# Chunk outputs of a Mamba-2 scan with tokens on the partitions, and the decays of its windows made beside the convolution

## What is computed

```python
z, xBC, dt = split(_rms(x, norm_w) @ in_proj_w)      # 512, 768, 8 channels
dt = softplus(dt + dt_bias)
xBC = silu(conv_b + sum(padded[:, k:k + L, :] * conv_w[:, k] for k in range(4)))
xh, Bm, Cm = split(xBC)                               # 8 heads x 64, 128, 128
def step(h, inp):                                     # over 512 tokens
    dec, u, bt, ct = inp                              # dec = exp(dt * A), u = dt * xh
    h = h * dec[:, :, None, None] + u[..., None] * bt[:, None, None, :]
    y = jnp.einsum('bhpn,bn->bhp', h, ct)
    return (h, y)
y = ys + D_skip * xh
out = x + _rms(y * silu(z), gnorm_w) @ out_proj_w
```

## Time and profile before

| | |
|---|---|
| time, median of 3 runs | 9226.33 us (9217.38 to 9246.14) |
| time of the profiled execution | 9249.62 us |
| its span | 9247.8 us |
| PE busy | 7938.6 us (86%) |
| PEld busy | 3524.7 us (38%) |
| DVE busy | 5014.7 us (54%) |
| ACT busy | 3326.8 us (36%) |
| POOL busy | 1960.8 us (21%) |
| mean granted clock of TensorE | 0.897 |

### The profile page before, as it was taken

How to read it: one execution, slowest core, us unless ns; L and a number is a source line. 1 busy time by engine, 2 the same in 40 slices (tenths; PEclk the granted TensorE clock), 3 DMA queues, 4 the chain that set the end, 5 groups by cost and what they waited for, 6 DMA issues and landing times.

```text
span 9247.8 us, 129067 instructions
## 1 busy us (share of the span) xinstructions
PE 7938.6 (86%) x37700; PEld 3524.7 (38%) x38020; DVE 5014.7 (54%) x12781; ACT 3326.8 (36%) x4038; POOL 1960.8 (21%) x1802
## 2 busy tenths in 40 slices
PE   3979799897998979889798897979989798897988
PEld 0343433434333343333434334343343433334343
DVE  3555364654645556454564656536465464555546
ACT  0424334242342424424243342433424234242442
POOL 3040130302203031130311304013030221303113
PEclk5989889898998989989799898989989899898998
DMA  3142231323313132041422303223131330313213
GB/s 73 20 74 35 41 60 20 65 33 48 53 19 70 28 57 51 12 75 23 69 39 26 71 17 69 35 43 57 20 69 30 50 58 12 70 28 64 45 19 72
DMA packets 216597, 421.47 MB, mean 46 GB/s; under 512 B 35542, under 2 KB 126584, under 8 KB 215812
## 3 DMA queue, kind: packets, MB, share of 16 engines
q1 hardware_dynamic: 213841, 412.14, 25.9%
q10 hardware_dynamic: 2048, 0.53, 0.0%
HBM read 190.14 MB, written 8.51 MB: 21 GB/s over the span
## 4 chain that ended last, share of the span: by engine, by line
PE 59%; issue 14%; DVE 13%; DMA 6%; POOL 4%; ACT 2%; SPq 2%; DVEq 0%; ACTq 0%; POOLq 0%
PE ps L1004 13%; PE ps L941 10%; PE ps L975 8%; PE ps L977 6%; PE ps L903 5%; DVE mx L1588 5%; PE ps L979 4%; PE ps L1009 4%; DMA stage<-in_mask 3%; PE ps L1124 2%; DMA qst<-q1hl 2%; PE ps L960 2%; PE ps L1040 2%; DVE xc L1716 1%; ACT PR L1362 1%
## 5 line engine op out<-in xcount | busy, mean ns | idle before, releaser
L1362 ACT ACTIVATE PR<-ps 128x1024 f32<-128x1024 f32 x2496 | 2504.0, 1025 | 2634.8 <-PE ps L977 1514.2
L1559 DVE CUSTOM_DVE_ANT_0 ps<-ps,maskq 128x402 f32<-128x402 f32 x4203 | 2408.3, 587 | 1567.1 <-PE ps L941 1375.8
L1004 PE MATMUL ps<-PR,vbuf 128*32 128x512 f32 x9984 | 1356.6, 616 | 5.2 <-ACT PR L1362 5.2
L977 PE MATMUL ps<-maskk,identb 128*128 128x512 bf16 x3008 | 1147.6, 382 | 0.0
L941 PE MATMUL ps<-kst,qst 96*128 96x402 bf16 (+1 forms) x3115 | 1026.0, 342 | 115.6 <-DVE mx L1559 89.9
L1588 DVE TENSOR_REDUCE mx<-ps 128x2 f32<-128x804 f32 x1024 | 933.3, 988 | 314.1 <-PE ps L960 312.7
L960 PE MATMUL ps<-kst,qst 100*128 100x402 f32 x2048 | 753.3, 495 | 360.8 <-DMA qst<-q1hl 254.4
L975 PE MATMUL ps<-qst,kst 99*128 99x512 bf16 x2496 | 956.7, 383 | 7.3
L979 PE MATMUL ps<-qst,kst 102*128 102x512 f32 x1664 | 768.0, 526 | 100.3 <-ACT PR L1362 71.0
L941 PEld LDWEIGHTS ps<-kst,qst 96*128 96x128 bf16 x3115 | 282.4, 97 | 1209.7 <-DVE mx L1559 819.4
L722 POOL MEMSET qst<- 3x2048 f32 (+1 forms) x34 | 47.5, 1398 | 3117.7 <-PE ps L1004 3071.1
(11 more groups left out here) (194 smaller groups left out, 8046.4 us busy)
## 6 DMA issues: line engine op xcount, KB each, us to landing
kst<-khl SPq DMA_DIRECT2D x96, 800.5 KB, 17.0
kst<-khl SPq DMA_DIRECT2D x300, 200.1 KB, 7.6
stage<-in_maskt SPq DMA_DIRECT2D x204, 256.0 KB
stage<-in_mask SPq DMA_DIRECT2D x204, 201.0 KB
ctxs<-in_ctxt SPq DMA_DIRECT2D x17, 1601.0 KB, 9.7
qst<-q1hl SPq DMA_DIRECT2D x96, 256.0 KB, 12.1
win_s<-in_w_in SPq DMA_DIRECT2D x16, 1288.0 KB, 5.9
KS<-khl SPq DMA_DIRECT2D x102, 200.1 KB
```

The lines of the kernel that those rows point to most:

```text
L977: mm = pe.matmul(o, identb[:, :], maskk[:, t, :], start=False, stop=True)
L1004: mm = pe.matmul(ps[32 * j:32 * j + 32, 6, :], l, PR[:, t % 2, j, :], start=(t == 0), stop=(t == KT - 1), tile_position=(0, 32 * j))
L1362: nc.scalar.activation(PR[:, t % 2, 2 * half:2 * half + 2, :], ps[:, 2 * half:2 * half + 2, :], ACT.Exp, scale=scale).then_inc(s_p, 1)
L1559: nc.vector.tensor_tensor_reduce(src, src, maskq[:, i, c0:c0 + w], 1.0, -3.0e38, ALU.add, ALU.max, mx[:, c, h * QT + i:h * QT + i + 1]).th ...
```

## The change

The chunk's output is now computed with tokens on the partitions. The 8 matmuls of a chunk have the window (128 x 128) as weights and 64 columns of `dx` to stream, and all write one bank. The state's part is one matmul (`s_zi`), scaled afterwards by a third column group of `dec`, so `Ce`, its exponential and its matmuls go. The skip term D x becomes four matmuls with a diagonal `dskd`. z is projected with tokens on the partitions as well. The gated output `ug` is squared by ACT with an accumulator, transposed by PE, copied by ACT and projected, block by block inside the chunk loop; the norm's one-column matmuls go.

All four `window_sums` and exponentials stand in the loop of the input projection; the windows lie in the space of `QS1`, and two DMAs (`rows_q1`) restore the constant rows there. Eight fills stand ahead of the transposes, one behind each j from 0 to 9 and three behind j = 10. The exponential of dt is ahead of the copies on ACT, and the convolution has three DVE instructions, as ACT makes the fourth tap. POOL makes the first four key parts after the RMS scale, and the rest between and behind the four `spread_a`. The LayerNorm has three DVE passes in place of four (with the square sum), and its RMS scale is made in two halves. The second LayerNorm, the transposes and q are split in three tiles and one. `spread` has four matmuls over all 128 rows, with no wait among them, and stands behind the first tile of `project_out`. On SP two mask pieces are loaded before x, and the other two after `stack_q1`.

```diff
+OUT_BANK = [5, 7, 6, 3]
+XT1_BANK = [2, 4]
+FILL0 = V_LN + 1
+FILL_AT = [1] * (NCH + XT) + [3]
+assert FILL0 + sum(FILL_AT) == KT + 2 * NC
...
+    def rows_q1(b):
+        sp.wait_ge(s_yp, LEAD + (b + 1) * QT)
+        alone(sp)
+        for g in range(G1):
+            sp.dma_start(f(QS1[g][KROWS1:MROW1 + 1, :, :]), qrows1.rearrange("r (h t) -> r h t", h=GH))\
+                .then_inc(s_qs1[g], 16)
...
-        sp.wait_ge(s_g, QT * (b + 1))
+        load_pieces(b, bn, 0, PIECE1, False)
+        sp.wait_ge(s_D, QT * (b + 1))
         alone(sp)
         load_xt(bn)
-        load_pieces(b, bn, 0, PIECE1, False)
         sp.wait_ge(s_vfree, (b + 1) * KT)
         alone(sp)
         load_ctx(bn)
+        rows_q1(b)
         for g in range(G1):
             stack_q1(b, g)
...
         def spread_a(c):
+            pool.wait_ge(s_a, b + 1)
             if c > 0:
                 pool.wait_ge(s_D, b * QT + c)
-                if c > 1:
-                    pool.wait_ge(s_cum, b * (QT - 1) + c - 1)
             nc.gpsimd.tensor_tensor(
                 aU[:, :, :], aa[:, c, :].unsqueeze(2).broadcast_to([P, HM, P]),
                 upto[:, :].unsqueeze(1).broadcast_to([P, HM, P]), ALU.mult).then_inc(s_au, 1)
         spread_a(0)
-        for c in range(QT):
+        spread_a(1)
+        spread_a(2)
+        parts(b, K1[NC])
+        spread_a(3)
+        for item in K1[NC + 1:]:
+            parts(b, item)
...
-        project_out(wo0_s, 0, G0 - 1, G0, G0 - 1)
-        fill(1)
+        project_out(wo0_s, 0, G0 - 1, G0, range(1))
+        spread(b, G0 - 1)
+        project_out(wo0_s, 0, G0 - 1, G0, range(1, QT))
         pe.wait_ge(s_norm, LEAD + b * NG + G0)
         project_out(wo0_s, G0 - 1, G0, G0)
-        fill(1)
-        fill(NC - 2 + V_LN)
+        fill(FILL0)
...
-            if j == NCH + 1:
+            if j == 4:
                 whole_decays(b)
-            elif j == NCH + 2:
-                window_sums(b, 0)
-            if j == 4:
                 pe.wait_ge(s_sp, b * SPN + 1)
...
             mm.then_inc(s_in, 1)
-        fill(V_IN)
+            fill(FILL_AT[j])
+            if NCH - 2 <= j < NCH + 2:
+                window_sums(b, j - NCH + 2)
+        assert not second
+        pe.wait_ge(s_xc, b * NCH + 2)
+        pe.wait_ge(s_vfree, (b + 1) * KT)
+        pe.wait_ge(s_rest, rests(b, K1[-1]) + 1)
+        for c in range(QT):
+            cs = slice(c * P, (c + 1) * P)
+            mm = pe.matmul(ps[:, 6, cs], xc[:, NCH - 2, cs], xc[:, NCH - 1, cs], start=True, stop=True)
+        mm.then_inc(s_G, 1)
+        for c in range(QT - 1):
+            cs = slice(c * P, (c + 1) * P)
+            mm = pe.transpose(ps[:, 7, cs], xc[:, NCH - 2, cs], ident[:, :])
+        mm.then_inc(s_bt, 1)
+        def x_tokens(c):
+            if c == 0:
+                pe.wait_ge(s_zs, b * XT + 1)
+                pe.wait_ge(s_xc, NCH * (b + 1))
+            else:
+                pe.wait_ge(s_dx, b * QT + c)
+            for i in range(XT):
+                mm = pe.transpose(ps[:, 1, i * P:(i + 1) * P], xc[:, i, c * P:(c + 1) * P], ident[:, :])
+            mm.then_inc(s_tok, 1)
+        def project_block(c):
+            pe.wait_ge(s_g, b * QT + c + 1)
+            if c == 0:
+                pe.wait_ge(s_zs, XT * (b + 1))
+            else:
+                pe.wait_ge(s_ut, b * QT + c)
+            for i in range(XT):
+                mm = pe.transpose(ps[:, 0, i * P:(i + 1) * P], ug[:, c % 2, i * P:(i + 1) * P], ident[:, :])
+            mm.then_inc(s_gt, 1)
+            pe.wait_ge(s_ut, b * QT + c + 1)
+            if c == 0:
+                pe.wait_ge(s_Ld, QT * (b + 1))
+            elif c == 1:
+                pe.wait_ge(s_btok, b + 1)
+            elif c == 2:
+                pe.wait_ge(s_GM, b + 1)
+            for k in range(XT):
+                mm = pe.matmul(ps[:, OUT_BANK[c], 0:D], yt[:, k, c * P:(c + 1) * P], wout_s[:, k, :],
+                               start=(k == 0), stop=(k == XT - 1))
+            mm.then_inc(s_op, 1)
+        x_tokens(0)
         for c in range(QT):
             cs = slice(c * P, (c + 1) * P)
             nb = b * QT + c
             if c > 0:
-                window_sums(b, c)
+                pe.wait_ge(s_h, LEAD + b * (QT - 1) + c)
+                if c == 1:
+                    pe.wait_ge(s_zs, b * XT + 3)
+                else:
+                    pe.wait_ge(s_ti, b * (QT - 1) + c - 1)
+                pe.matmul(ps[:, 3, :], xc[:, NCH - 1, cs], Hst[:, :], start=True, stop=True).then_inc(s_zi, 1)
...
+                pe.wait_ge(s_zs, b * XT + 2)
+                pe.wait_ge(s_dskd, b + 1)
+            elif c == 1:
+                pe.wait_ge(s_g, nb)
+            else:
+                pe.wait_ge(s_tj, b * (QT - 1) + c - 1)
             for i in range(XT):
...
-            fill(1)
+                pe.matmul(ps[:, 2, i * P:(i + 1) * P], xc[:, i, cs], dskd[:, i, :], start=(i == 0), stop=False)
             pe.wait_ge(s_M, nb + 1)
             pe.wait_ge(s_dx, nb + 1)
...
             for h in range(HM):
-                i, e = h // 2, h % 2
-                o = ps[64 * e:64 * e + 64, 2, i * P:(i + 1) * P]
-                mm = pe.matmul(o, dx[:, h * PD:(h + 1) * PD], Ld[:, h, :], start=True, stop=(c == 0),
-                               tile_position=(0, 64 * e))
-                if c > 0:
-                    mm = pe.matmul(o, Hst[:, h * PD:(h + 1) * PD], Ce[:, h, :], start=False, stop=True,
-                                   tile_position=(0, 64 * e))
+                mm = pe.matmul(ps[:, 2, h * PD:(h + 1) * PD], window(c)[:, h, :], dx[:, h * PD:(h + 1) * PD],
+                               start=False, stop=(h == HM - 1))
             mm.then_inc(s_yp, 1)
             if c < QT - 1:
+                x_tokens(c + 1)
...
+                pe.matmul(ps[:, 4, :], btok[:, c, :], dx2[:, :], start=True, stop=True).then_inc(s_hp, 1)
+            if c > 0:
+                project_block(c - 1)
+        pe.wait_ge(s_ti, (b + 1) * (QT - 1))
+        project_block(QT - 1)
...
+                mm = pe.transpose(ps[:, XT1_BANK[k], i * P:(i + 1) * P], xs1[:, i, k * P:(k + 1) * P], ident[:, :])
+            if i >= QT - 2:
+                mm.then_inc(s_xst1, 1)
+            if i == QT - 2:
+                pe.wait_ge(s_xn1, 2 * DT * b + DT)
+                for item in LASTQ:
+                    project_q1(item, 0, i * P + P)
+        pe.wait_ge(s_xn1, 2 * DT * (b + 1))
         for item in LASTQ:
-            project(b, item, pj_bank[item], None)
+            project_q1(item, (QT - 1) * P, T).then_inc(s_proj, 1)
...
     def window_decays(b, c):
-        nb = b * QT + c
-        act.wait_ge(s_D, nb + 1)
-        act.wait_ge(s_yp, LEAD + nb)
-        nc.scalar.activation(Ld[:, :, :].rearrange("p h t -> p (h t)"),
+        act.wait_ge(s_D, b * QT + c + 1)
+        nc.scalar.activation(window(c).rearrange("p h t -> p (h t)"),
                              ps[:, 4:6, :].rearrange("p a n -> p (a n)"), ACT.Exp).then_inc(s_Ld, 1)
...
+            nc.scalar.activation(xc[:, ch, :], ps[:, bank, :], ACT.Identity, bias=cb_c[:, ch:ch + 1],
+                                 scale=cw_c[:, ch * TAPS + TAPS - 1:(ch + 1) * TAPS])
             nc.scalar.activation(rawc[:, n % 2, TAPS - 1:TAPS - 1 + T], ps[:, bank, :], ACT.Copy)\
                 .then_inc(s_rawcp, 1)
...
+        act.wait_ge(s_sp, b * SPN + 2)
+        nc.scalar.activation(sp_t[:, 2, :], sp_t[:, 1, :], ACT.Exp).then_inc(s_spe, 1)
...
+        for n in range(NCH):
+            gate(n)
+            if n + 2 < NCH:
+                copy_raw(n + 2)
+            fill(FILL_AT[n + 3])
+            if n == 0:
+                act.wait_ge(s_dps, b + 1)
+                nc.scalar.activation(dec[:, :, :].rearrange("p a n -> p (a n)"),
+                                     ps[:, 4, 0:3 * QT * HM], ACT.Exp).then_inc(s_dec, 1)
+            elif n <= QT:
+                window_decays(b, n - 1)
...
+        for c in range(QT):
             act.wait_ge(s_g, b * QT + c + 1)
-            cs = slice(c * P, (c + 1) * P)
-            nc.scalar.activation(zs[:, :, cs], yt[:, :, cs], ACT.Square).then_inc(s_g2, 1)
...
+            nc.scalar.activation(th[:, c % 2, :], ug[:, c % 2, :], ACT.Square, accum_out=ssq[:, c:c + 1])\
+                .then_inc(s_g2, 1)
+            act.wait_ge(s_gt, b * QT + c + 1)
+            nc.scalar.activation(yt[:, :, c * P:(c + 1) * P], ps[:, 0, :].rearrange("p (a n) -> p a n", a=XT),
+                                 ACT.Copy).then_inc(s_ut, 1)
...
         for i in range(QT):
+            nc.vector.scalar_tensor_tensor(out=xres[:, i, :], in0=xres[:, i, :], scalar=moments[:, i, 0:1],
+                                           in1=lng_s[:, :], op0=ALU.subtract, op1=ALU.mult).then_inc(s_ln[0], 1)
+        dve.wait_ge(s_rstd, b + 1)
+        dve.wait_ge(s_ln[0], QT * (b + 1))
+        for i in range(QT):
```

## The result

The changed kernel takes 8695.89 us (median of 4 runs, 8694.80 to 8698.13) against 9225.26 us (4 runs of the kernel before; the 9226.33 of the table ahead is the median of three of them): a ratio of 0.942, 95% interval 0.941 to 0.944. The profiled execution spans 8693.3 us, so its 16 batches take 543.3 us each against 578.0 before, 34.7 less.

A forecast was written before the change was run, and what follows sets the result against it. The prediction took PE as the bound (59% of the chain) and counted its waits: 10.0 - 18.7 + 18.3 + 8.7 + 5.8 = 24.1 us a batch, 386 in 16, so 9226 - 386 = 8840 us, range 8640 to 9000.

The forecast's parts named there:

- Head: Layer 0's end to dt: covered reciprocal, shorter spread, LayerNorm by tiles; 10.0 us a batch gained, bounds 8 and 12.
- Projection and convolution: Layer 1's input projection: PE the bound, ACT's fifth key waits for the stack; 18.7 us a batch lost, bounds 3 and 25.
- Scan and tail: First scan matmul to q ready: chunks of 8.5 us for 11.4; 18.3 us a batch gained, bounds 10 and 24.
- the 3 us for a low clock: Scan and tail: allowance for a low clock in the tail and narrow matmuls in the chunks, raising 46.1 to 49.1 us.
- The fear that narrow matmuls bring the clock down: Rival: PE falls to 1.2 GHz from the scan to q, 34 us more a batch, 9384 us; chance 0.04.
- q: PE's wait for q's DMAs: context and two mask pieces leave their way; 8.7 us a batch gained, bounds 4 and 12.
- The rest: Batch's end and layer 0's groups: shorter spreads, covered reciprocal, clock; 5.8 us a batch gained, bounds 3 and 8.
- The stack lands in time: Rival beside the convolution: key stack there when ACT needs it, 11.0 us a batch given back, 8665 us; chance 0.15.
- The clock stays at 2.4 GHz: Rival: no low PE clock in the convolution, scan and tail, 9.9 us a batch given back, 8682 us; chance 0.15.
- Chunks stay a chain, or q waits for the context: Rival: chunks take 11.4 us, or the context delays q; 8.7 us a batch lost either way, 8980 us; chance 0.19.

The follow-up runs named there:

- key_less: Changed kernel with the last of the first key stack's three DMAs copying one head of four (a quarter of its bytes): 8601.0 us.
- k_last: Changed kernel with the second four key projections behind all values and POOL's fourth window-sum input ahead of their parts: 8555.4 us.
- win_half: Changed kernel with each of the scan's 64 window matmuls streaming 32 columns instead of 64: 8867.2 us.
- before_sp: Kernel before the change, with only SP's queue altered: context issued once the values are taken, two mask pieces instead of four ahead of q: 9156.5 us.
- narrow: Changed kernel with the spread of the reciprocals back to 32 rows, one row group after the other: 8922.6 us.
- no_cover: Changed kernel with all of `project_out` behind the spread again, in both layers: 8773.6 us.
- rms_once: Changed kernel with POOL's first half of the RMS norm waiting for the squares of all four tiles: 8779.0 us.
- ctx_late: Changed kernel with the context issued behind the constant rows, directly ahead of q's wait, some 25 us later: 8696.6 us.

## Why the prediction was right, and where it was not

*Head, 10.0 forecast, 12.8 measured.* The reciprocal, the spread and `project_out` were counted at 3.4. From the last group's sums to DVE's first addition the head took 13.6 us before and 7.2 after, so 6.4. The prediction left out the clock: it was 0.75 in this stretch before and is 1.00 after:

```profile
2689.70:2703.32 13.62, 12.28 (x47) 9.63 (x48) 1.64 (x2) 0.39 (x1) 0.58 (x2) 0.75 0.00 0
```

```profile
2542.36:2549.53 7.17, 7.17 (x43) 6.29 (x44) 1.64 (x2) 0.00 (x0) 0.00 (x0) 1.00 0.00 0
```

The LayerNorm by tiles was closer: from that addition to the transposes 17.6 us before and 10.5 after, 7.1 less where 5.6 was counted; from there to dt it grew by 0.7, where 1.0 less was counted.

*Projection and convolution, -18.7 forecast and measured.* The mechanism is right: PE is the bound, the fifth key waits for the stack, POOL's fourth input is queued behind it, PE's fourth window sum behind that, and this sum starts 43.0 us into the stretch, where 43.1 was counted. (The fourth key part's terms there, 9.8, 4.4 and 2, add up to 16.2 and not 16.4.) That the loss agrees to a tenth is luck. PE reaches the wait 2 us sooner, so the stall is 10.4 us for 8.5, and PE's work outside it takes 47.4 us where 49.8 was counted, 42.7 of instructions and 7 for the clock. `key_less` and `k_last` show that the stall is real and is worth 8.8 us a batch. The Trainium skill ("DMA: Bandwidth & Descriptors", section Bandwidth) has 341 GB/s for 1 MB from HBM to 128 partitions; by an estimate from this figure the stack would land in 7 us. The trace does not agree for this transfer, which goes from SBUF to 32 partitions: its last DMA landed 22.3 us after its issue, with 2.4 MB in all. The context is a transfer from HBM; it landed in 6.8 us when nothing ran beside it, 1601 KB or 241 GB/s.

*Scan and tail, 18.3 forecast, 23.1 measured.* A chunk takes 7.9 us where 8.5 was counted (its terms add up to 8.4), and the fourth block is projected 33.8 us into the stretch, not 35.4. From there to the end of q are 10.6 us, and 10.7 were counted before the 3 us for a low clock. So these 3 us are the larger mis-sized term: the clock is 1.00 in the scan and 0.96 over the whole stretch. The fear that narrow matmuls bring the clock down was not wrong but early, as `win_half` shows.

*q, 8.7 forecast, 6.8 measured.* The queue on SP is the cause (`before_sp`), and PE's wait for q's DMAs is 9.7 us and not 8.

*The rest, 5.8 forecast, 11.7 on the mean.* This is the term that was sized worst. It had 4.2 us for shorter spreads and a covered reciprocal and 1.6 for the clock. By the means of the batches the groups of layer 0 gained 5.8 us, the part of layer 1 behind its first scores 3.3, and the first scores themselves 2.6, where nothing was counted. In these three stretches together PE's time at half fell from 52 to 38 us a batch. That is worth at most half, 7 us, where 1.6 was counted, and 4.2 + 7 is close to the 11.7. Over the whole batch the time at half fell from 119 to 79 us; 5 of these 40 lie in the wait for q, where PE is idle and they cost nothing. `narrow`, `no_cover` and `rms_once` show the same thing backwards: a microsecond of wait or of narrow matmuls put back costs two to four. No run holds the clock and changes only the instructions, so the split between the two stays an estimate.

*The rivals.* "The stack lands in time" gave 8665, nearer to the measured time than the forecast's 8840, and it is wrong: ACT waits 11.3 us. "The clock stays at 2.4 GHz" (8682) is the nearer in kind, but only the 3.0 us that it had in the scan and tail came in part; beside the convolution the clock stayed low (0.85), and where it rose, in the head and in the rest, little or nothing was counted. "Chunks stay a chain, or q waits for the context" is excluded by the 7.9 us and by `ctx_late`. Whoever checks this forecast by its total alone would pick the wrong story: 8696 comes from a stall that exists and a clock gain that was not counted.

## What to carry to other kernels

Before a wait or a narrow form is priced by its own microseconds, look at PE's clock in the stretches behind it: here each microsecond of wait or of narrow matmuls put back cost two to four. When a move makes one engine wait in program order for a DMA, list what is queued behind it on that engine; taking the second four key projections behind the values, with no byte less, took a 10 us stall away. And judge a forecast by its stretches, not by its sum.

## What the runs showed of the hardware that was not expected

- Less streaming made PE slower: 32 instead of 64 columns in 64 matmuls with full weights left each at 0.117 us at full clock, and the clock fell from 1.00 to a mean of 0.80 in the scan shown (`win_half`).
- The context's DMA landed after 25.7 us when it was issued behind the second key stack, 7.3 us after the stack, and after 6.8 us alone (`ctx_late`).
- The key stack's landing goes with its bytes: its last DMA landed 22.3 us after its issue with 2.4 MB in the stack and 16.0 us with 1.8 MB (`key_less`), some 110 GB/s from 128 partitions to 32 at a time.
